# Loading x in pairs of blocks with a cap on those under way, with the last region's stores on two queues, in a two-dimensional mixing kernel

## The reference, cut to what matters

```python
# stage 1: x (1, 16, 1024, 1024); a bias from the distance q - k, through a hidden layer of 32
rel = tril(idx[:, None] - idx[None, :])
nd = log(|c * rel| + 1) / (log(|c * pos| + 1) + EPS)         # pos: by row
h = relu(nd[..., None] * W1[0] + b1)
x = x + (einsum('qkm,mh->qkh', h, W2) + b2).transpose(2, 0, 1)
# stage 2: the 16 channels are mixed at every point (t, s)
ret = einsum('BGMTS,GMN->BGNTS', x, w + eye)
ret += (x mixed by a 16x16 matrix of rank 2 + diagonal that depends on the row t)       # qw1, qw2, qdd
ret += (x mixed by a 16x16 matrix of rank 2 + diagonal that depends on the column s)    # kw1, kw2, kdd
```

## Time and profile before

| | |
|---|---|
| median of 3 runs | 933.41 us (924.12 to 935.43) |
| profiled execution | 934.25 us, its span 932.4 us |
| PE busy | 745.9 us, 80% |
| DVE, ACT, POOL busy | 452.0, 385.9, 433.6 us |
| DMA moved | 149.63 MB, mean 160 GB/s |
| granted clock of PE, mean | 0.931 |

### The profile page before, as it was taken

The page is one execution under the profiler, slowest core; times in us unless marked ns, Lnnn a source line. Parts: engine busy times, 40 slices in busy tenths (PEclk is TensorE's granted clock), DMA queues, the critical chain, the costliest instruction groups (busy, mean ns, idle before and its releaser), DMA issues.

```text
span 932.4 us, 39068 instructions
## 1 busy us (share of the span) xinstructions
PE 745.9 (80%) x18210; PEld 546.7 (59%) x18210; DVE 452.0 (48%) x483; ACT 385.9 (41%) x412; POOL 433.6 (47%) x267
## 2 busy tenths in 40 slices
PE   0676856897779767987899788988789988998972
PEld 0154645676557555755577556655457656767972
DVE  7595523473437524754256333644336533653442
ACT  3969425633554335534343334324343335431100
POOL 3645422362326413555378545755448845860010
PEclk9879978998999989999899989989999999998997
DMA  6786689379956997399917997389825996486099
GB/s 136 180 174 148 148 182 210 88 153 225 209 139 125 242 192 172 72 202 231 207 29 152 210 195 172 47 188 235 204 49 111 230 247 144 75 193 146 12 187 159
DMA packets 300798, 149.63 MB, mean 160 GB/s; under 512 B 29788, under 2 KB 296412, under 8 KB 300636
## 3 DMA queue, kind: packets, MB, share of 16 engines
q1 hardware_dynamic: 181536, 89.17, 44.1%
q10 hardware_dynamic: 119100, 57.97, 28.0%
HBM read 77.61 MB, written 69.47 MB: 158 GB/s over the span
## 4 chain that ended last, share of the span: by engine, by line
PE 71%; issue 13%; SPq 4%; ACT 3%; DMA 3%; ACTq 2%; DVE 2%; POOL 1%; POOLq 0%
PE main L746 27%; PE main L735 25%; PE bias L760 19%; SPq L324 3%; ACTq L268 1%; DMA homes<-in_x 1%; ACT homes L504 1%; ACT hidden L493 1%; POOL hidden L454 1%; DMA out_mixed<-homes 1%; DVE homes L297 1%; SPq L337 1%; DMA b_mats<-homes 0%; DVE w_blocks L617 0%; SPq L268 0%
## 5 line engine op out<-in xcount | busy, mean ns | idle before, releaser
L454 POOL TENSOR_TENSOR hidden<-log_table,row_scale 128x1024 f32<-128x1024 f32 x192 | 365.9, 1921 | 356.6 <-PE bias L760 348.8
L746 PE MATMUL main<-homes,mats_b 32*32 32x120 f32 (+1 forms) x9216 | 280.1, 268 | 95.2 <-issue 75.0
L493 ACT ACTIVATE hidden<-hidden,b_col 128x1024 f32<-128x1024 f32 x192 | 218.9, 1148 | 309.3 <-POOL hidden L454 157.2
L746 PEld LDWEIGHTS main<-homes,mats_b 32*32 32x32 f32 x9216 | 252.9, 132 | 159.5 <-issue 132.7
L735 PEld LDWEIGHTS main<-homes,mats_a 32*32 32x32 f32 x8192 | 241.6, 129 | 89.7 <-issue 70.5
L735 PE MATMUL main<-homes,mats_a 32*32 32x128 f32 x8192 | 265.1, 277 | 28.8 <-issue 28.4
L660 DVE SCALAR_TENSOR_TENSOR homes<-bias,b_col,homes 64x512 f32<-64x512 f32 (+1 forms) x256 | 185.9, 747 | 117.7 <-PE bias L760 88.1
L760 PE MATMUL bias<-hidden,w_blocks 128*64 128x512 f32 x768 | 212.0, 654 | 26.4 <-ACT hidden L493 10.7
L642 DVE TENSOR_TENSOR homes<-main,homes 128x1024 f32<-128x1024 f32 x128 | 156.7, 1225 | 116.2 <-PE main L735 113.6
L632 DVE COPY homes<-main 128x960 f32<-128x960 f32 x64 | 74.1, 1158 | 225.3 <-PE main L746 222.0
L520 ACT ACTIVATE homes<-main 128x960 f32<-128x960 f32 (+1 forms) x80 | 71.1, 891 | 123.0 <-PE main L746 116.6
(11 more groups left out here) (37 smaller groups left out, 31.1 us busy)
## 6 DMA issues: line engine op xcount, KB each, us to landing
out_mixed<-homes ACTq DMA_DIRECT2D x204, 192.0 KB
homes<-in_x SPq DMA_DIRECT2D x200, 192.0 KB, 5.9
homes<-in_x SPq DMA_DIRECT2D x72, 256.0 KB, 7.0
out_mixed<-homes ACTq DMA_DIRECT2D x72, 128.0 KB
homes<-in_x SPq DMA_DIRECT2D x136, 64.0 KB
mats_in<-a_mats SPq DMA_DIRECT2D x128, 64.0 KB
out_mixed<-homes ACTq DMA_DIRECT2D x32, 256.0 KB
out_mixed<-homes SPq DMA_DIRECT2D x32, 256.0 KB
```

Source lines behind the costliest of these rows:

```text
L454: nc.gpsimd.tensor_tensor(hidden_tile(u, g).rearrange("p (j s) -> p j s", j=ROWS), bass.AP(logs.tensor, logs.offset, [list(logs.ap[0]), [1 ...
L493: nc.scalar.activation(hidden_tile(u, g), hidden_tile(u, g), ACT.Relu, bias=b1_col[:, 0:1])\
L746: mm = pe.matmul(main[of_group(g), i % 2, j * W:j * W + REGION_TILES[k] * ROWS], b_weights(g, C * ROWS + j), y_column(k, g, C * ROWS + j), ...
```

## The change

Loads of x: the 8 blocks of a piece are now 4 pairs, and semaphore x_in[q] belongs to pair q of every piece. Before SP issues a pair it waits until an earlier pair has landed: the one four pairs back for regions 0 and 1, the one two pairs back from region 2 on. ACT and DVE wait for all four pairs at the first tile of a piece (`wait_for_x`), and no longer at each of its tiles.

Stores: SP's half of a region's last piece (`store_upper`) moves ahead of the x piece at step 13 (in region 0 ahead of a chunk and x(2,0) at step 7), and still waits for the region's last tile. In the last region the pieces are 2, 3, 3, 3, 2, 1, 1 tiles, and ACT and SP take four blocks of each.

```diff
+LAST_STORES = (2, 3, 3, 3, 2, 1, 1)
+PAIRS = 4
+OPEN_PAIRS = 4
+MIXING_PAIRS = 2
-        x_in = [sem(f"x_in{i}") for i in range(6)]
+        x_in = [sem(f"x_in{q}") for q in range(PAIRS)]
...
         def store_pieces(k):
-            return STORE_PIECES[REGION_TILES[k]]
+            return LAST_STORES if k == REGIONS - 1 else STORE_PIECES[REGION_TILES[k]]
...
-        def x_landed(k, T):
+        LOAD_ORDER = [(0, 0), (0, 1), (0, 2)] + [(1, i) for i in range(6)]
+        for k in range(2, REGIONS):
+            LOAD_ORDER += [(k, i) for i in range(6)]
+        def wait_for_x(eng, k, T):
             i = piece_of(load_pieces(k), T)
-            return x_in[i], times(LOAD_PIECES, i, k) * PER_PIECE
+            if T == piece_start(load_pieces(k), i):
+                for landed in x_in:
+                    eng.wait_ge(landed, (LOAD_ORDER.index((k, i)) + 1) * GS * DMA)
...
-        def is_last(k, i):
-            return i == len(store_pieces(k)) - 1
+        def is_shared(k, i):
+            return k == REGIONS - 1 or i == len(store_pieces(k)) - 1
...
-                for b in BLOCK_ORDER:
-                    sp.dma_start(home_rows(b, x_slot(k, T), n * ROWS),
-                                 x[0, :, t0:t0 + n * ROWS, b * W:(b + 1) * W]).then_inc(x_in[i], DMA)
+                for q in range(PAIRS):
+                    earlier = LOAD_ORDER.index((k, i)) * PAIRS + q - (OPEN_PAIRS if k < 2 else MIXING_PAIRS)
+                    if earlier >= 0:
+                        sp.wait_ge(x_in[earlier % PAIRS], (earlier // PAIRS + 1) * GS * DMA)
+                    for b in BLOCK_ORDER[q * GS:(q + 1) * GS]:
+                        sp.dma_start(home_rows(b, x_slot(k, T), n * ROWS),
+                                     x[0, :, t0:t0 + n * ROWS, b * W:(b + 1) * W]).then_inc(x_in[q], DMA)
...
+            def store_upper(k, i):
+                taken, count = emptied(a_tile(k, piece_start(store_pieces(k), i + 1) - 1))
+                sp.wait_ge(taken, count)
+                for b in BLOCK_ORDER[sum(SHARED_PORTIONS):]:
+                    store_block(sp, k, i, b).then_inc(out_done[i], DMA)
...
+                    if k + 1 < REGIONS and T == REGION_TILES[k] - 2:
+                        store_upper(k, len(store_pieces(k)) - 1)
+                    if k == REGIONS - 1:
+                        for i in range(len(store_pieces(k))):
+                            if T == piece_start(store_pieces(k), i + 1) - 1:
+                                store_upper(k, i)
                     if k + 2 < REGIONS and T in (7, 10, 13):
                         load_x(k + 2, loaded[k + 2])
                         loaded[k + 2] += 1
-                last = len(store_pieces(k)) - 1
-                taken, count = emptied(a_tile(k, REGION_TILES[k] - 1))
-                sp.wait_ge(taken, count)
-                for b in BLOCK_ORDER[sum(LAST_PORTIONS):]:
-                    store_block(sp, k, last, b).then_inc(out_done[last], DMA)
...
         def add_const_bias(k, T):
-                landed, count = x_landed(k, T)
-                act.wait_ge(landed, count)
+                wait_for_x(act, k, T)
```

More of the change, by code:

```diff
@@ L29 @@
 STORE_PIECES = {8: (2, 3, 3), 15: (2, 3, 3, 3, 4)}
+LAST_STORES = (2, 3, 3, 3, 2, 1, 1)
 LOAD_PIECES = {8: (1, 3, 4), 15: (1, 3, 3, 3, 4, 1)}
+PAIRS = 4
+OPEN_PAIRS = 4
+MIXING_PAIRS = 2
 PORTIONS = (3, 3, 2)
-LAST_PORTIONS = (2, 2)
+SHARED_PORTIONS = (2, 2)
 CHUNK = 32
@@ L142, in build @@
         main_taken = [sem(f"main_taken{i}") for i in range(2)]
-        out_done = [sem(f"out_done{i}") for i in range(5)]
+        out_done = [sem(f"out_done{i}") for i in range(len(LAST_STORES))]
         def tile_of(k, T):
@@ L213, in times @@
         def times(pieces, i, k):
-            return sum(i < len(pieces[REGION_TILES[r]]) for r in range(k + 1))
+            return sum(i < len(pieces(r)) for r in range(k + 1))
         def store_pieces(k):
-            return STORE_PIECES[REGION_TILES[k]]
+            return LAST_STORES if k == REGIONS - 1 else STORE_PIECES[REGION_TILES[k]]
         def load_pieces(k):
@@ L268, in store_block @@
             return eng.dma_start(out[0, :, t0:t0 + n, b * W:(b + 1) * W], home_rows(b, mixed_slot(k, T), n))
-        def is_last(k, i):
-            return i == len(store_pieces(k)) - 1
+        def is_shared(k, i):
+            return k == REGIONS - 1 or i == len(store_pieces(k)) - 1
         def portions_of(k, i):
-            return LAST_PORTIONS if is_last(k, i) else PORTIONS
+            return SHARED_PORTIONS if is_shared(k, i) else PORTIONS
         def portion_blocks(k, i, p):
@@ L316, in load_x @@
                 if k >= 1 and T + 1 >= HOME_TILES:
-                    sp.wait_ge(out_done[0], times(STORE_PIECES, 0, k - 1) * PER_PIECE)
+                    sp.wait_ge(out_done[0], times(store_pieces, 0, k - 1) * PER_PIECE)
                 elif k >= 2 and T + 1 < REGION_TILES[k - 2]:
                     left = piece_of(store_pieces(k - 2), min(T + n, REGION_TILES[k - 2] - 1))
-                    sp.wait_ge(out_done[left], times(STORE_PIECES, left, k - 2) * PER_PIECE)
+                    sp.wait_ge(out_done[left], times(store_pieces, left, k - 2) * PER_PIECE)
                 t0 = tile_of(k, T) * ROWS
-                for b in BLOCK_ORDER:
-                    sp.dma_start(home_rows(b, x_slot(k, T), n * ROWS),
-                                 x[0, :, t0:t0 + n * ROWS, b * W:(b + 1) * W]).then_inc(x_in[i], DMA)
+                for q in range(PAIRS):
[5 more added lines that the diff above has]
+                                     x[0, :, t0:t0 + n * ROWS, b * W:(b + 1) * W]).then_inc(x_in[q], DMA)
             def load_mats_a(v):
@@ L395, in _ @@
                         loaded[k + 2] += 1
-                last = len(store_pieces(k)) - 1
-                taken, count = emptied(a_tile(k, REGION_TILES[k] - 1))
-                sp.wait_ge(taken, count)
-                for b in BLOCK_ORDER[sum(LAST_PORTIONS):]:
-                    store_block(sp, k, last, b).then_inc(out_done[last], DMA)
-            for i in range(5):
-                sp.wait_ge(out_done[i], times(STORE_PIECES, i, REGIONS - 1) * PER_PIECE)
+            for i in range(len(out_done)):
+                sp.wait_ge(out_done[i], times(store_pieces, i, REGIONS - 1) * PER_PIECE)
         @block.gpsimd
@@ L649, in add_bias @@
                 u = tile_of(k, T)
-                landed, count = x_landed(k, T)
-                dve.wait_ge(landed, count)
+                wait_for_x(dve, k, T)
                 if u:
```

## The result

| | before | changed | |
|---|---|---|---|
| median | 934.42 us (924.12 to 937.04, 4 runs) | 959.24 us (949.5 to 976.22, 4 runs) | ratio 1.026, 95% interval 1.0169 to 1.0352 |
| profiled execution, span | 932.4 us | 961.0 us | |

The change makes the kernel 2.6% slower.

The account below looks back on a forecast made before the run. It took PE, stopped by instructions arriving late behind x and stores, as the bound. 934.25 - 52 (cap) + 3 (late x) + 9 (region 0) - 5.5 (last stores) = 888.8, so 889 us; range 866 to 945.

Parts of the forecast that it names:

- What bounds the kernel: PE's matmuls: PE stops only while DMAs run, taken as instructions arriving late behind x and stores; 35.4 us idle under x alone.
- The queue ahead of an instruction transfer shrinks by about 2 us: From region 2 on, four x DMAs out mean 3.9 us of work in place of 6, a cut the size of the stops.
- 52 us of the sum: Gain from capping x: 28 us of stops and 5 of clock under x alone, 14 and 5 in mixed stretches.
- Rival (b): PE's stops don't depend on depth, as DMA engines take turns between queues; the cap saves nothing: 941 us, chance 0.15.
- The round under x alone, 5.0 and 6 us: SP's queue: two pairs of x take 5.0 us to issue and land at 192 KB, 6 us at 256 KB.
- The other rounds: SP's queue: 6.2 us for a round of 64 KB, and 7 us for one of 192 KB with stores.
- A queue with 7 us of air: SP's queue in each region: 88 us of work in a region of 95 us, so x seldom comes late.
- the charge of 3 us: Cost of x's second piece coming later in each region, as PE only now and then stands; bounds 0 to 15 us.
- Rival (c): SP's queue becomes the bound from region 2 on if a mean round exceeds 7.0 us; 1007 us at 8.0, chance 0.14.
- Region 0, 9 us lost (6 to 12): SP, on the chain there, waits 5.8 us for tile 7's add before storing; the cap's rounds add 3 us.
- The last region, 5.5 us gained: Final stores on both queues, ending in single tiles, finish at 927 in place of 932.4 us; gain 2 to 8.
- The clock: PE's granted clock rises as stops go: 5 us back under x alone and 5 us in mixed stretches.

Follow-up runs that it names:

- experiment 8: Kernel before, but x of regions 5 to 8 loaded as one row of each block and piece, 32 MB less read: ratio 0.95, 872.26 us.
- Experiment 7: Changed kernel with two pairs under way only in the fourth and fifth x piece from region 2 on, four elsewhere: 1.0151 of the kernel before, 929.27 us.
- experiment 1: Kernel before with the pairs and the cap alone, stores as before: median 944.72 us against 919.68, no interval.
- experiment 2: Kernel before with only SP's half of a region's last output piece stored ahead of x: ratio 1.0079, 921.7 us.

## Why the prediction was wrong, by its own steps

**What bounds the kernel** was read rightly: PE stops while DMAs run, experiment 8 shows that x causes a large part of it, and the packets show that late instructions are the link. Two readings on the way were not sound. The 43 + 85 = 128 matmuls of the earlier trace rows are one step of the column products, cut in two by a stop; they say nothing of the spacing, which has to be counted from stop to stop. And one of the five stretches "nearly without DMA", 376 to 398 us, had 81 GB/s: PE did not stop there either, so it takes more than some traffic.

**"The queue ahead of an instruction transfer shrinks by about 2 us"** is the step that failed, and with it 52 us of the sum. By the packets the wait shrank from 3.9 to 3.3 us, 0.6 and not 2 (0.3 to 0.6 against all traces without a cap); 2 us would indeed have been enough, as the one pair shows with 1.6 us and hardly a stop. And x was spread over more blocks, so that all stops together went from 110.2 to 103.1 us only. Experiment 7 has no recovery at all. I took the landing time of 6.1 us for a queue, as 128 KB in the empty setup had landed in 3.0 us. That pair of rows compares two kinds of DMA: the 3.0 us belong to another tensor and to two thirds of the bytes. The rows to compare were of one size at two depths. The kernel before had only a hint: no x DMA whose landing it shows took under 5.0 us (median 6.4). Measured, the landing of 192 KB goes from 5.9 us without a cap to 5.9 at two pairs and 5.4 at one.

Rival (b), at 0.15, described this part better than the forecast did, though its 941 us missed the cost of the cap. The Trainium skill (DMA: Bandwidth & Descriptors, Queues, rings and completion order) says that each engine takes turns between its queues by packet. From no cap to two pairs the traces come near that (3.9 to 3.3 us); at one pair the DMA engines are also busy only half of the time, so the 1.6 us can come from less depth or from less traffic, and no run tells the two apart. How long a turn is, and so why the wait is 3 to 4 us, no run here shows.

**The round under x alone, 5.0 and 6 us**, is a term that was mis-sized, for the same reason: 6 rounds took 40.6 us, 6.8 each, where I had 32. The other rounds were right: 6.0 to 6.6 us against 6.2 for 64 KB, and 12.6 us for 2 rounds with stores (10.1 to 18.1 over the regions) against 14. The sum for SP's queue was 88 us; 4 x 6.6 + 12.6 + 40.6 + 17 makes 97, more than the 95 us that the forecast gave a region.

**"A queue with 7 us of air"** was a step that failed too. A mean does not say when a piece is needed. SP is released for a batch by a tile of the row phase (its chunk of matrices waits for POOL, which waits for PE), and the pieces of this batch are then needed at fixed steps of PE. From the first x of a batch to the second piece it is 27.7 to 29.9 us now and was 18.4, as I had it; but to the end of the fifth piece it is 90.3 us (317.65 to 407.95) and was 67.7 (507.42 to 575.15). DVE sees this at each piece, though SP has air at the end of the round. PE's lead of 7 us past a late add did not hide it: the charge of 3 us stands against 98 us more of DVE's waits, 36 us more of PE's waits for ACT and DVE, and 15 to 25 us of time in experiment 1. Rival (c) named the place and the mechanism; its price was for a mean round over 7.0 us, while the loss began at a mean of (4 x 6.6 + 12.6 + 40.6) / 12 = 6.6, for the reason just given.

**Region 0, 9 us lost (6 to 12)**: right in its mechanism, and a little too small. From the first issue of x(1,5) to the landing of x(2,1) it was 117.51 to 149.97, 32.5 us; now it is from 120.91 us to 166.4, 45.5: 13 us lost with the cap, just over the 12, since the three rounds cost some 7 us where I had 3. In experiment 2, without the cap, 7 us (1 to 13) of time, near the 5.8 us of idle time.

**The last region, 5.5 us gained**: right. 13.9 us to 8.0 in the profile is 5.9 us; alone it gave 0.9%, 8 us (3 to 13).

**The clock**, 10 us of the 52: not recovered, as the stops stayed. Its mean is 0.925 now and was 0.931, and PE's busy time rose by 10.5 us.

In the sum: 934.25 + 9 + 4 for region 0, - 5.9 at the end, and some 20 us for the other regions make 961; the 20 us are what is left over and not a measurement, with late x and the 10.5 us of busy time both in them. The profiled execution took 962.83 us.

## What to carry to other kernels

Before you cap the transfers under way, measure the landing time of one DMA of that size with little beside it. If it is about that of many, it is latency and not a queue: the cap then sets a rate of so many DMAs for each landing, and the way from harmless to costly is one step (three pairs 0.998, two 1.026, one 1.41). Sum such a queue not by its mean share of a period but from the event that releases it to each use. And a cap that shortens a wait a little but makes the traffic last longer can leave the sum of the waits where it was.

## What the runs showed of the hardware that I had not expected

- The landing time of a DMA of 16 partitions in rows of 512 bytes goes with its size, hardly with what is under way: 3.6, 5.4 and 7.6 us for 64, 192 and 256 KB with two out from region 2 on; 5.9 and 7.0 us for the last two sizes with five to seven out. A DMA of 8 KB took 3.1 us (experiment 8).
- PE's stops without a semaphore are waits for its next 16 KB of instructions, one for every 128 matmuls: 62 of 69 stops end 1.1 to 1.7 us after the end of such a packet. Under x alone the packet starts some 3.9 us after PE has come into a block, where it is 0.3 us when nearly no DMA runs.
- A stream of x of 139 to 165 GB/s idles PE for as large a share of the time (17%) as one of 188 to 202 GB/s (15%).
- Leaving out 32 of 150 MB of loads, which no engine had waited for at that place, made the kernel 5% faster.
